# The one-column bf16 product in front of each group of corner products, left out of a three-layer kernel on TensorE

## Time and profile before

| | |
|---|---|
| runs shown | 669.65, 669.99, 670.72 us |
| profiled execution, its own time | 671.73 us |
| its span, first to last instruction | 669.9 us |
| granted TensorE clock, mean | 0.900 |
| TensorE busy | 558.8 us (83%) |
| VectorE busy | 494.3 us (74%) |
| ScalarE busy | 353.0 us (53%) |

### The profile page before, as it was taken

One profiled execution on the slowest core, in us unless ns is written; L12 is line 12 of the kernel. 1 busy time (PEld: TensorE's weight loads), 2 busy tenths in 40 slices (PEclk: granted clock), 3 DMA queues, 4 the chain that ended last, 5 costly groups with the idle time before them and its releaser, 6 DMA issues.

```text
span 669.9 us, 15018 instructions
## 1 busy us (share of the span) xinstructions
PE 558.8 (83%) x6324; PEld 374.1 (56%) x6324; DVE 494.3 (74%) x1126; ACT 353.0 (53%) x530; POOL 53.0 (8%) x45
## 2 busy tenths in 40 slices
PE   4588889999999999999999999999886930015998
PEld 2235346576576667667666765766765830014536
DVE  5769887788877878887787888778551399996422
ACT  1656665685596568559656855965233333331230
POOL 2010000100100010010001001000000015500120
PEclk9979989999999999999999999999695975555798
DMA  5001121102101210210121021010010030000001
GB/s 147 0 0 42 24 56 23 21 14 61 26 1 24 55 21 15 60 26 1 24 55 21 14 61 26 1 24 16 20 26 2 1 133 0 0 1 0 0 1 63
DMA packets 49674, 18.57 MB, mean 28 GB/s; under 512 B 39100, under 2 KB 48328, under 8 KB 49608
## 3 DMA queue, kind: packets, MB, share of 16 engines
q1 hardware_dynamic: 49608, 17.62, 11.1%
HBM read 14.46 MB, written 3.15 MB: 26 GB/s over the span
## 4 chain that ended last, share of the span: by engine, by line
PE 69%; DVE 23%; ACT 5%; issue 2%; DMA 1%; SPq 0%; ACTq 0%
PE bank L1056 16%; DVE acc L731 8%; PE bank L1103 5%; PE bank L1018 4%; PE bank L1221 4%; PE bank L1299 4%; PE bank L1225 3%; PE bank L1122 3%; PE bank L1231 3%; PE bank L1237 3%; PE bank L1180 3%; PE bank L1106 2%; PE bank L1233 2%; PE bank L1235 2%; PE bank L1100 2%; PE bank L1339 2%
## 5 line engine op out<-in xcount | busy, mean ns | idle before, releaser
L731 DVE SCALAR_TENSOR_TENSOR acc<-bank,cw,acc 128x508 f32<-128x508 f32 (+2 forms) x240 | 176.2, 738 | 44.0 <-ACT acc L494 39.7
L1056 PE MATMUL bank<-xnT,wq 128*128 128x512 f32 x320 | 156.1, 615 | 16.4 <-DVE acc L731 16.0
L1056 PEld LDWEIGHTS bank<-xnT,wq 128*128 128x128 f32 x320 | 56.9, 193 | 76.7 <-issue 45.5
L494 ACT ACTIVATE acc<-bank,cw 128x512 f32<-128x512 f32 x80 | 55.5, 694 | 48.0 <-PE bank L1056 47.3
L1103 PE MATMUL bank<-kq 128*128 128x384 f32 x128 | 50.7, 499 | 0.2
L1018 PE MATMUL bank<-cst,kT 128*128 128x128 f32 x16 | 3.9, 428 | 52.3 <-DVE kT L942 52.3
L509 ACT ACTIVATE vT<-acc 128x512 f32<-128x512 f32 x32 | 21.4, 675 | 46.1 <-DVE acc L731 46.0
L762 DVE SCALAR_TENSOR_TENSOR AM<-bank,rb,DT 128x384 f32<-128x384 f32 x64 | 37.4, 605 | 1.8 <-PE bank L1103 1.5
L437 POOL TENSOR_TENSOR Yc<-T 128x256 f32<-128x256 f32 x7 | 4.3, 611 | 402.6 <-PE bank L1194 402.6
L824 DVE SCALAR_TENSOR_TENSOR xres<-bank,f,xres 128x256 f32<-128x256 f32 x64 | 26.9, 477 | 10.3 <-PE bank L1225 10.0
L540 ACT ACTIVATE T<-bank 64x512 f32<-64x512 f32 x16 | 9.5, 592 | 44.8 <-PE bank L1122 33.7
(11 more groups left out here) (237 smaller groups left out, 1202.1 us busy)
## 6 DMA issues: line engine op xcount, KB each, us to landing
wq<-in_w_qkv SPq DMA_DIRECT2D x8, 640.0 KB, 4.0
blocks<-AM SPq DMA_DIRECT2D x128, 8.0 KB, 1.6
xres<-in_x SPq DMA_DIRECT2D x2, 512.0 KB, 4.4
Yl<-in_y_init SPq DMA_DIRECT2D x8, 128.0 KB, 2.2
Bl<-blocks SPq DMA_DIRECT2D x8, 128.0 KB, 2.0
wg<-in_w_gate SPq DMA_DIRECT2D x8, 128.0 KB, 2.2
solved<-Yl SPq DMA_DIRECT2D x8, 128.0 KB, 2.1
Yc<-solved SPq DMA_DIRECT2D x64, 16.0 KB, 1.9
```

Source lines behind the costliest of these rows:

```text
L494: a(acc[:, u % RING, :, :], bank[6 + u % 2][:, :].rearrange("p (b l) -> p b l", b=4), ACT.Copy, scale=cw[:, t, 3:4]).then_inc(s_tap.next(f ...
L731: stt(w, ps[:, :, 0:L - s], cw[:, t, 3 - s:4 - s], w, ALU.mult, ALU.add).then_inc(s_cv.next(f"u{u}_{s}"), 1)
L1056: ins = mm(bank[6 + u % 2][:, :], wq[:, cc, t, :], xnT[:, cc, 512 * half:512 * half + 512], start=cc == 0, stop=cc == KC - 1)
```

## The change

The function `carry` and its nine call sites (80 calls as the program runs) are taken out. The waits stay where they are, and the last wait in front of a group now rides on the group's first corner product. `segb` stays, since L1097 and L1101 read it.

```diff
-            def carry(ps):
-                mm(ps[:, 0:1], segb[:, 0, :], segb[:, 0, 0:1], start=True, stop=True)
...
                 if name in ("ca", "cs"):
                     half = int(name == "cs")
-                    if not half:
-                        carry(ps)
...
                 if name in ("ta", "tb"):
-                    carry(ps)
                     for ch in range(CH):
...
                 elif name == "lt":
-                    carry(ps)
...
                 elif name == "ly":
-                    carry(ps)
...
                 elif name in ("mt0", "my1"):
-                    carry(ps)
...
                 elif name == "mm":
                     py = fill(post, "my0", h)
-                    carry(ps)
-                    carry(py)
...
                 elif name in ("sa", "rs"):
                     half = int(name == "rs")
-                    if not half:
-                        carry(ps)
```

## The result

The changed kernel takes 674.76 us, median of five runs (672.77 to 675.38), against 669.65 for the kernel before beside it: ratio 1.0065, 95% interval 1.0043 to 1.0087. The prediction was 667.2, with 0.05 on slower. One execution of e6, which took 983.05 us at a mean granted clock of 0.554, is left out of its median and ratio.

A forecast was written before the change was run, and what follows sets the result against it. TensorE was taken to bound the middle heads, with the chain alternating between engines in the last two. Savings of 0.1 + 1.5 + 0.15 + 1.05 = 2.8 us take the median from 669.99 to 667.2 us, range 665.9 to 668.9.

The forecast's parts named there:

- (a): 51 groups behind a busy whole-array product: removing the one-column product saves 0.002 us each on average, 0.1 us in all.
- Rivals 2: Corner load is pulled under the running product, saving 0.09 us more at 57 groups: 662.1 us; chance 0.05.
- 4 (0.56): Waits on corner loads, checked only after the array drains, add 0.04 us at 57 groups: 669.5 us; chance 0.11.
- (b): 6 groups where `ca` follows `rs`, both 128 x 32: joining them saves 0.25 us each, 1.5 us in all.
- (c): 6 `mm` groups with two removed products on a busy TensorE: 0.025 us saved each, 0.15 us in all.
- (d): Nine groups in the last two heads, TensorE idle and waiting: corner load takes the removed load's place, 1.05 us saved.
- It is all on the chain: The whole 2.8 us saving lies on the chain; only VectorE in mid-head could take part of it back.
- rival 1: In middle heads a late VectorE result absorbs part of the gain, keeping the head's old length: 668.7 us; chance 0.14.
- No DMA, no other engine's instruction and no order of steps changes.: Whole program: removing the products was claimed to leave DMA, other engines and step order unchanged; no time was assigned.
- Rival 3: Last two heads: more of the stretch falls to half clock, slower; with 5 us of it, 672.2 us; chance 0.06.

The follow-up runs named there:

- e6: Changed kernel with `lt`'s first two pairs of corner products run three times, 16 instructions more a head: 674.08 us, ratio 1.0049 to the kernel before.
- e8: Kernel before with only `ca`'s one-column product replaced by two wait instructions: 669.09 us, ratio 0.9973.
- e1: Kernel before with all 80 one-column product calls replaced by two satisfied waits each, instruction numbers kept: 667.45 us against 670.86, ratio 0.9956.
- e9: As e1, but 17 waits a pass instead of 20 and two small products before the first head: 667.65 us, ratio 0.9950 to the kernel before.
- e10: The changed kernel as it stands, timed again on another chip: 674.0 us against 670.96 for the kernel before, ratio 1.0051.
- e7: As e6, plus four small corner products (16 instructions) once before the first head: 667.64 us, ratio 0.9956 to the kernel before.
- the twins: e6 and e7, the same work per head, the second with 16 instructions more once before the first head: 674.08 and 667.64 us.
- e3: Changed kernel with 60 more TensorE instructions (satisfied waits) once before the first head: 677.97 us, ratio 1.0107 to the kernel before.
- e4: Changed kernel with 17 more satisfied waits in each pass, making a pass 1,536 instructions: 681.13 us, ratio 1.0159 to the kernel before.
- e2: Kernel before, products kept, with 200 more satisfied waits on TensorE once before the first head: 689.6 us, ratio 1.0285.

## Why the prediction was wrong

Its steps, in its order:

- (a), 51 groups at 0.002: right (0.004 by the records). L1051 to the corner load is 0.52 with the product gone, so the passage costs 0.09 with or without it. Rivals 2 (0.43) and 4 (0.56) are out.
- (b), 6 x 0.25: right, by the changed profile (1.88) and by e8's heads (58.34 for 58.58).
- (c), 0.34 to 0.31: right.
- (d), the corner load in the place of L1015's: right as far as the rows show it; no run isolates its 1.05. The sum of the four, 2.8 us, lies within what e1 measures with the numbers kept, 670.86 - 667.45 = 3.4, or 1.9 to 4.0 by the interval, and near the 3.3 of the fairer pair, before and e9; each undisturbed middle head is 0.29 shorter (58.29) where 0.28 was said.
- "It is all on the chain", and rival 1: right. No new idle time behind VectorE; a `tb` that ends late does move the head's end by its whole stop, as a TensorE saving does.
- **The step that failed: "No DMA, no other engine's instruction and no order of steps changes."** TensorE's own program became shorter, and with it the position of each 16 KB block changed against the work. The queue that fetches the blocks is on the page before (q8, 50 packets), I counted the removed product in time and not in instructions, and I had no term for it. Its price is 6.5 us of stops for 0.9 before, 5.6 us more in the profiled execution (8.6 us of stops in e10's), against 2.8 saved. 5.6 - 2.8 = 2.8 us slower; the medians of the two timings say 5.1 and 3.0. The profiled execution itself shows only 1.1 (671.0 for 669.9 us of span), because it got a mean clock of 0.97 in its first 100 us where before's got 0.93 and began `ta` of head 0 at 102.76 instead of 104.72.
- Rival 3 (slower by the clock) got 0.06 and is not the cause. The half-clock stretch is 10.2 us as before in the first profile of the changed kernel, which has all the stops. It is 13.6 in e10's, but 13.6 or 13.7 also in e7's and e8's, which are faster than before. The sign came out as that rival's, the cause did not.

It was foreseeable in kind, not easily in sign. Before's own trace had one such stop, 0.31 us in `tb` of head 0 (a group of 128 small products that takes 1.58 where the others take 1.26), at the deepest boundary that it had, 46. With 20 instructions fewer in a pass and boundaries that so far moved 3 a pass, "what do the boundaries hit now" had an answer in the count of instructions.

What stays open: how the stops in `lt` depend on what came before (e1 has five, e7 one, at depths of `ta` that overlap), and why the packet's start, its length and the time to its use vary from one execution to the next; other DMA traffic beside the fetch is a candidate that was not tested. That the late fetch is the cause and not only in step with the stop rests on the order in time (packet end, then 1.2 to 1.6 us, then the array) in all 42 cases, on the 588 pairs without an exception, and on the twins; nothing was tried that delays a packet by itself.

## What to carry to other kernels

When an edit changes how many instructions an engine has, price that as well: find the stretch in which instructions are eaten fastest (here 256 in 1.2 us within a group, and in 2.6 with the products between, groups of fp32 corner products at 4 instructions each), count where the 256-instruction blocks fall in it before and after, and look for stops "<-issue" inside groups that have no wait. A result of half a per cent, good or bad, in a kernel with such groups may be the position and not the edit; a twin with the instruction count restored tells them apart. And a position that does well is worth keeping on purpose: a few cheap instructions in idle time, and a pass of a whole number of blocks. Before a total is taken as proof of a sum, split it: here the part behind the last head alone is 3.7 us shorter in e1's profiled execution than in the changed kernel's.

## What the hardware showed that I had not expected

- A 16 KB block of instructions comes as one packet of 0.9 to 1.5 us, and where the array waited for it, it went on 1.2 to 1.6 us after that packet had ended. From packet start to use it is 2.15 us at the least, in 588 of 588.
- No fetch in these twelve profiles is more than one block ahead; three boundaries within 3.7 us of work cost 1.9 us at the third (e3, head 1).
- A wait on a semaphore that was reached long ago costs nothing visible where it replaces the one-column product behind a running long product (e1: 0.29 less a head, all of the predicted gain), but 0.106 us each in a row by the records, which shows before an idle array (17 cost 1.39 us in e4; 200 in e2).
- Joining two groups of the same tile size removes both passages between them: 0.25 us, 1.88 for 2.13 from `sa` to the product behind `cs`, in the changed kernel, in e1 and in e8.
